# An expert layer computed on every token, changed to one computed on the chosen experts' rows, in a whole decoder layer

## The chip, the core and the metric

The kernel runs on one core of a Trainium2 chip, in one launch. The metric is device time in microseconds (us) of one execution. The core's engines run at the same time and meet at semaphores: TensorE (PE in the profile; PEld is its loading of weights), VectorE (DVE), ScalarE (ACT), GpSimd (POOL) and SyncE (SP), which here only issues transfers (DMAs).

## The reference

The input is 32 sequences of 256 tokens of width 256. Each goes through three residual layers: self attention with rotary embedding (16 heads of 64), cross attention to a context of 256 tokens (16 heads of 64, with a mask on the query rows), and a mixture of 8 experts:

```python
x = x + attention(layernorm(x))
x = x + cross_attention(layernorm(x), ctx, mask)
h = layernorm(x)
probs = softmax(h @ Wg)                       # 8 experts
top_vals, top_idx = top_k(probs, 2)
gates = top_vals / sum(top_vals)
expert_out = einsum('th,ehd->etd', h, We) + be
x = x + sum over the two chosen experts of gate * expert_out
```

All is fp32. The kernel splits each operand of a projection into a high and a low part (`fp32r`) and sums three products of them (`pieces`).

## The kernel before

One sequence is one batch, `b`. The program is a software pipeline: `body(b)` goes through 36 slots, and each engine has its own list of what it does in a slot, in an order that is written out by hand. An engine executes its list strictly in that order. A head takes one slot: self heads 0 to 15 in slots 0 to 15, cross heads 16 to 31 in slots 20 to 35. In slots 16 to 19 no head begins (`DRAIN`); there the self attention's output is projected, added, normalised and turned.

What a head does: `scores` (PE, two heads in every even slot, into two PSUM banks), `row_maximum` (DVE), `exponentials` (ACT), `reciprocal` (DVE), the multiplication by it (POOL, L1150, one slot later), `turn_probs` (PE, L648, two slots later), `pT_out` (ACT) and `values` (PE, L665). `scores` of the next two heads waits until the exponentials of the last one are done (in cross attention until DVE has copied the scores). Every fourth head, `oT_out`, `oT_low` and `project` (PE, L690) follow.

Everything else is a unit in the table `UNITS`: slot, kind, index, the batch it works for (0, the next or the one before) and whether ACT and DVE treat it in that slot or the next (`NOW`, `LATE`). Kinds Q, K and V are projections; the Q and K of self attention also take three operations of POOL each (L1158, L1162, L1139), in slots 30 to 9. L1, L2 and L3 are the turns after the three normalisations, LG the gate logits, GT and BI the expert biases.

EX is the expert layer of the batch before, as eight units in slots 8 to 19: each multiplies 128 tokens by the matrices of two experts (`tile_product`, L546, six matmuls of 512 columns), and DVE adds both halves, weighted by `gates`, to `x1` (L1021). All 8 experts are computed on all 256 tokens, and `gates` is zero for the six that were not chosen. BI adds the biases, and SP stores `x1` to the output. The matrices of all experts lie in SBUF from batch 0 on.

SP's list in a batch is short: the context in slot 9, the mask, two small loads, the output in slot 20 and the next input in slot 22. After batch 31 comes `body(32)`, with no heads: only the expert layer of batch 31.

## Time and profile before

| | |
|---|---|
| median of 3 runs | 3581.41 us (3578.99 to 3582.03) |
| span of the profiled execution, first to last instruction | 3581.8 us |
| that execution's own time | not given apart from the span; the page has only the span |
| PE busy | 3501.3 us, 98% |
| DVE, ACT, POOL busy | 66%, 62%, 59% |
| one steady batch | 109.3 us: the same operation (`rstd` of slot 24) begins at 1000.02 and at 1109.33 us |

A steady batch in the trace: slot 24 begins at about 1000 us, slot 0 at about 1036, slot 8 at about 1057, slot 12 at about 1069, slot 16 at about 1078 and slot 20 at about 1097. In a row of the page, `xN` is a count, the two numbers behind the first bar are the busy time in us and the mean duration in ns, and behind the second bar stands the idle time of the engine before them and who ended it. In a timeline row come the start and the duration in us (of all, where it has a count), the engine, the line and the operation, and in brackets the engine's idle time before it and who ended it. A windows row has the length of the stretch, then the busy time of PE, PEld, DVE, ACT and POOL, the granted clock as a share of 2.4 GHz, the DMA share and GB/s.

### The profile page before, as it was taken

How to read it: one execution, taken by the hardware profiler on the slowest of the kernel's cores; microseconds unless marked ns; L12 is line 12 of the kernel's file. 1: busy time of each engine (PE TensorE's matmuls, PEld its weight loads, DVE VectorE, ACT ScalarE, POOL GpSimd, SP SyncE). 2: the span in 40 equal slices, each digit the busy share in tenths (PEclk: the TensorE clock that was granted, in tenths of full speed). 3: DMA queues.
4: the chain of work that ended last, by engine and by line, in shares of the span. 5: the costliest groups of instructions: out<-in, count | busy, mean ns of one | idle time of the engine just before them, and what ended most of it. 6: DMA issues, size and time to landing. Idle time of an engine off the chain costs nothing.

```text
span 3581.8 us, 80997 instructions
## 1 busy us (share of the span) xinstructions
PE 3501.3 (98%) x28992; PEld 2949.8 (82%) x28992; DVE 2358.7 (66%) x7401; ACT 2220.8 (62%) x6442; POOL 2121.2 (59%) x1928
## 2 busy tenths in 40 slices
PE   6899999999999999999999999999999999999998
PEld 5788888888888888888888888888888888888886
DVE  6666667666666666676666666666766667666665
ACT  5666666666666666666666666666666666666663
POOL 5555676555665556765556755566655567555662
PEclk8999999999999999999999999999999999999999
DMA  3100000000000000000000000000000000000000
GB/s 98 37 10 13 10 10 10 10 13 12 7 10 12 9 12 10 9 10 10 12 12 7 10 12 10 12 10 9 10 10 12 12 7 12 11 10 12 13 6 8
DMA packets 46796, 47.44 MB, mean 13 GB/s; under 512 B 8256, under 2 KB 43328, under 8 KB 46400
## 3 DMA queue, kind: packets, MB, share of 16 engines
q1 hardware_dynamic: 45696, 41.99, 4.0%
q8 instruction: 236, 3.87, 0.4%
q14 instruction: 160, 1.31, 0.1%
q10 hardware_dynamic: 704, 0.27, 0.0%
HBM read 33.86 MB, written 8.39 MB: 12 GB/s over the span
## 4 chain that ended last, share of the span: by engine, by line
PE 89%; DVE 5%; ACT 2%; issue 2%; POOL 2%; DMA 0%; ACTq 0%; POOLq 0%; DVEq 0%
PE unit_ps L536 19%; PE pT_ps L648 14%; PE oT_ps L665 14%; PE score_ps L632 11%; PE unit_ps L524 10%; PE wo_ps L690 10%; PE unit_ps L546 8%; DVE x L1021 1%; ACT probs L798 1%; POOL probs L1150 1%; DVE probs L936 1%; PE unit_ps L555 1%; DVE bn L863 1%; DVE x_in L1029 1%; ACT v_sb L744 1%
## 5 line engine op out<-in xcount | busy, mean ns | idle before, releaser
L1150 POOL TENSOR_TENSOR probs<-probs,inv_sum 128x512 f32<-128x512 f32 x1024 | 1062.1, 1041 | 956.4 <-DVE inv_sum L919 956.3
L787 ACT ACTIVATE pT<-pT_ps 128x512 f32<-128x512 f32 x1024 | 606.2, 594 | 136.1 <-PE pT_ps L648 135.5
L798 ACT ACTIVATE probs<-probs,neg_max 128x256 f32<-128x256 f32 x1024 | 508.9, 500 | 276.4 <-DVE probs L936 276.4
L648 PE MATMUL pT_ps<-ident,probs 128*128 128x128 f32 x4096 | 634.0, 279 | 13.2 <-POOL probs L1150 12.5
L648 PEld LDWEIGHTS pT_ps<-ident,probs 128*128 128x128 f32 x4096 | 451.8, 141 | 221.8 <-issue 204.0
L798 ACT ACTIVATE probs<-score_ps,neg_max 128x256 f32<-128x256 f32 x1024 | 476.6, 476 | 179.1 <-DVE neg_max L925 179.1
L665 PE MATMUL oT_ps<-pT,v_sb 128*64 128x256 f32 x4096 | 556.0, 392 | 4.4 <-ACT pT L787 4.0
L936 DVE TENSOR_SCALAR_CACHE_REDUCE probs<-score_ps,mask_add 128x256 f32<-128x256 f32 x1024 | 433.4, 480 | 104.8 <-PE score_ps L632 101.9
L536 PE MATMUL unit_ps<-xs_hi,w_lo 128*128 128x256 f32 x1536 | 460.1, 300 | 9.3 <-DVE swap L972 7.8
L536 PE MATMUL unit_ps<-xs_hi,w_hi 128*128 128x256 f32 x1536 | 436.6, 284 | 0.0
L536 PE MATMUL unit_ps<-xs_lo,w_hi 128*128 128x256 f32 x1536 | 436.1, 284 | 0.0
L632 PE MATMUL score_ps<-k_hi,q_both 64*128 64x256 f32 x4096 | 387.1, 278 | 0.0
L925 DVE TENSOR_REDUCE neg_max<-score_ps 128x2 f32<-128x512 f32 x512 | 328.2, 682 | 88.7 <-PE score_ps L632 84.4
L665 PEld LDWEIGHTS oT_ps<-pT,v_sb 128*64 128x64 f32 x4096 | 248.8, 136 | 148.1 <-ACT pT L787 5.2
L632 PE MATMUL score_ps<-k_lo,q_both 64*128 64x256 f32 x2048 | 343.0, 331 | 15.6 <-ACT probs L798 8.7
L1162 POOL TENSOR_TENSOR rope<-rope,swap 128x512 f32<-128x512 f32 x256 | 331.4, 1295 | 20.1
L1158 POOL TENSOR_TENSOR swap<-swap,sin_sb 128x512 f32<-128x512 f32 x256 | 332.3, 1298 | 13.3 <-DVE swap L972 13.3
L1021 DVE SCALAR_TENSOR_TENSOR x<-unit_ps,gates,x 128x256 f32<-128x256 f32 x512 | 247.3, 483 | 109.3 <-PE unit_ps L546 98.8
L632 PEld LDWEIGHTS score_ps<-k_hi,q_both 64*128 64x128 f32 x4096 | 316.9, 186 | 0.0
L807 ACT ACTIVATE oT_hi<-oT_ps 128x512 fp32r<-128x512 f32 x256 | 153.1, 598 | 264.1 <-PE oT_ps L665 264.1
L744 ACT ACTIVATE v_sb<-unit_ps 128x512 f32<-128x512 f32 x256 | 152.4, 595 | 262.5 <-PE unit_ps L524 261.3
L536 PEld LDWEIGHTS unit_ps<-xs_hi,w_lo 128*128 128x128 f32 x1536 | 296.0, 193 | 20.9 <-issue 12.2
(121 smaller groups left out, 8573.0 us busy)
## 6 DMA issues: line engine op xcount, KB each, us to landing
x_in<-dram_x SPq DMA_DIRECT2D x32, 256.0 KB, 2.7
xn<-dram_ctx SPq DMA_DIRECT2D x32, 256.0 KB, 2.7
layer_out<-x SPq DMA_DIRECT2D x32, 256.0 KB, 2.2
swap<-dram_bout SPq DMA_DIRECT2D x32, 128.0 KB, 3.1
rope<-dram_be SPq DMA_DIRECT2D x32, 64.0 KB, 2.9
rope<-dram_we SPq DMA_DIRECT2D x5, 256.0 KB, 2.8
probs<-dram_sk SPq DMA_DIRECT2D x4, 256.0 KB, 5.1
x<-dram_cq SPq DMA_DIRECT2D x4, 256.0 KB, 3.2
```

The lines of the kernel that those rows point to most:

```text
L524: last = nc.tensor.matmul(ps[:, t * GW:(t + 1) * GW], a[:, c, t * P:(t + 1) * P], w[:, m, cols:cols + GW], start=n == 0, stop=n == 3 * NC - 1)
L536: last = nc.tensor.matmul(ps[:, j * T:(j + 1) * T], w[:, m, cols:cols + P], a[:, c, :], start=n == 0, stop=n == 3 * NC - 1)
L632: last = nc.tensor.matmul(score_ps[(s + i) % 2][:, t * T:(t + 1) * T], q_both[own, g % 2, q, cols], k[own, g % 2, c, :], start=n == 0, sto ...
L648: last = nc.tensor.transpose(pT_ps[s % 2][:, k * T + t * P:k * T + (t + 1) * P], probs[:, hs % P_BUFS, t, k * P:(k + 1) * P], ident[:])
L665: last = nc.tensor.matmul(oT_ps[i * HD:(i + 1) * HD, (hl // 2) * T:(hl // 2 + 1) * T], v_sb[:, g % 2, k, (hl + i) * HD:(hl + i + 1) * HD], ...
L690: last = nc.tensor.matmul(wo_ps[:, t * D:(t + 1) * D], o[:, c, t * P:(t + 1) * P], w[:, m, cols:cols + D], start=gg == 0 and t == 0 and c ...
L787: nc.scalar.activation(flat(pT[:, s % 2, :, :]), pT_ps[s % 2][:], ACT.Copy).then_inc(pT_ready.sem, 1)
L798: last = nc.scalar.activation(dst, src, ACT.Exp, bias=neg_max[:, h % STATS, t:t + 1], scale=1.0 if h < H else -1.0, accum_out=row_sum[:, h ...
L936: last = nc.vector.tensor_scalar(probs[:, s % P_BUFS, t, :], ps[:, t * T:(t + 1) * T], mask_add[:, t:t + 1], None, ALU.subtract, ALU.min, ...
L1150: nc.gpsimd.tensor_tensor(weights, weights, inv.unsqueeze(2).to_broadcast([P, NT, T]), ALU.mult).then_inc(probs_ready.sem, 1)
L1158: nc.gpsimd.tensor_tensor(swap[:], swap[:], sin_sb[:].unsqueeze(1).to_broadcast([P, NC, T]), ALU.mult).then_inc(sin_done.sem, 1)
L1162: nc.gpsimd.tensor_tensor(rope[:, n % 2, :, :], rope[:, n % 2, :, :], swap[:], ALU.add).then_inc(roped.sem, 1)
```

## The change

The expert layer no longer works batch by batch. The sequences fall into five groups (0 to 8, 9 to 17, 18 to 25, 26 to 29, 30 and 31). For each sequence:

- after the gates, DVE makes a one-hot table, PE counts by two small matmuls how many earlier tokens of the group chose each expert (unit RK, slot 11), and DVE makes from it the row of each of a token's two copies in a DRAM table that has a stretch of rows for each expert (`rows`);
- POOL scatters the normalised tokens to these rows, by four indirect DMAs of 128 rows of 1 KB in slot 13 (`scatter`);
- `x1` (with the biases) is stored to a DRAM tensor `x1_all` where it was stored to the output.

When a group is complete, DVE makes a list of its tiles of 128 rows with one expert each (`list_tiles`, slot 14). Two tiles are a pair; the groups have 22, 22, 20, 12 and 8 pairs, 84 in all. SP loads a pair's rows and its two expert matrices (512 KB each) with four DMAs, whose addresses it reads from the list; PE turns the rows (TT), ACT and DVE split them, PE multiplies (TM, twelve matmuls of 256 columns), ACT copies out, and SP stores the result rows with two DMAs. 69 pairs stand in batches 10 to 15, 19 to 24 and 27 to 31 (three, four or five in each), five in `body(32)`, and ten behind it.

For the sums, SP loads `x1` back, POOL gathers for each half of a sequence the 128 rows of either choice (two indirect DMAs), DVE adds both, weighted, to `x1_back`, and SP stores that to the output. `y_rows` and `x1_back` have one buffer each. 22 sequences are summed in batches 16 to 29 and 31, four in `body(32)`, and six behind it. A batch's first sum gathers in slots 0 and 4, its second in 8 and 12, the third in 20 and 24, the fourth in 28 and 32.

In batches 0, 2, 4 and 6, SP clears the four DRAM tables of 19,456 rows of 1 KB, in 36 DMAs each. SBUF no longer holds the expert matrices; they are split and stored to DRAM in batch 0.

```diff
+GROUPS = ((0, 9), (9, 18), (18, 26), (26, 30), (30, 32))
+CAP = max(e - b for b, e in GROUPS) * T
+ROWS = E * (CAP + P)
...
+LIST_AT = 14
+PAIRS_IN = {10: (0, 4), 11: (0, 4), 12: (0, 4), 13: (0, 4), 14: (0, 3), 15: (0, 3),
+            19: (1, 4), 20: (1, 4), 21: (1, 4), 22: (1, 4), 23: (1, 3), 24: (1, 3),
+            27: (2, 5), 28: (2, 5), 29: (2, 5), 30: (2, 5), 31: (3, 5), 32: (3, 5)}
+SUMS_IN = {**{b: 1 for b in range(16, 25)}, 25: 2, 26: 2, 27: 2, 28: 2, 29: 1, 31: 4, 32: 4}
+GATHER_AT = (0, 4, 8, 12, 20, 24, 28, 32)
+
...
-    9: [("EX", 1, -1, LATE)],
+    8: [("V", 2, 0, LATE), ("TT", 0, 0, NOW)],
+    9: [("TM", 0, 0, LATE)],
     10: [("V", 3, 0, NOW)],
-    11: [],
-    13: [],
-    14: [("EX", 3, -1, NOW)],
+    11: [("RK", 0, -1, LATE), ("TT", 1, 0, NOW)],
+    12: [("TM", 1, 0, LATE)],
+    13: [("TT", 2, 0, NOW)],
+    14: [("TM", 2, 0, LATE)],
     15: [],
     16: [],
-    17: [("K", 4, 0, NOW), ("EX", 4, -1, NOW)],
-    18: [("GT", 0, -1, NOW), ("EX", 5, -1, NOW), ("EX", 6, -1, LATE), ("V", 4, 0, NOW), ("L2", 0, 0, LATE)],
-    19: [("K", 5, 0, NOW), ("Q", 4, 0, NOW), ("EX", 7, -1, NOW)],
+    17: [("K", 4, 0, NOW), ("TT", 3, 0, NOW)],
+    18: [("GT", 0, -1, NOW), ("TM", 3, 0, NOW), ("TT", 4, 0, NOW), ("V", 4, 0, NOW), ("L2", 0, 0, LATE)],
+    19: [("K", 5, 0, NOW), ("Q", 4, 0, NOW), ("TM", 4, 0, NOW)],
     20: [("BI", 0, -1, LATE)],
     21: [("Q", 5, 0, LATE)],
...
+            def clear_rows(i, s):
+
+                blocks = range(s * ROWS // P // SLOTS, (s + 1) * ROWS // P // SLOTS)
+                sp.wait_ge(consts, 8)
+                sp.dma_start((x_rows + y_all)[i][blocks[0] * P:(blocks[-1] + 1) * P, :].rearrange("(n p) d -> p n d", p=P),
+                             y_tile[:, 0, :].unsqueeze(1).to_broadcast([P, len(blocks), D])).then_inc(cleared[i], 16)
...
+            def load_pair(n):
+
+                g = group_of_pair(n)
+                sp.wait_ge(list_ready, g + 1)
+                if n >= 2:
+                    sp.wait_ge(tiles_done, n - 1)
+                for i in range(2):
+                    at = tile_of_pair(n) + i
+                    sp.dma_start(x_tile[:, n % 2, i, :],
+                                 x_rows[g % 2][bass.ds(row_at(n, i), P), :]).then_inc(x_tile_in[n % 2], 16)
+                    expert = sp.value_load(tile_list[at:at + 1, g, 1:2], min_val=0, max_val=E - 1)
+                    sp.dma_start(w_tile[:, n % 2, i, :, :, :].rearrange("p h c n -> p (h c n)").bitcast(F32),
+                                 we_all[bass.ds(expert, 1), :, :].rearrange("e p n -> p (e n)")) \
+                        .then_inc(w_tile_in[n % 2], 16)
...
+            def store_pair(n):
+
+                g = group_of_pair(n)
+                if g >= 2:
+                    sp.wait_ge(half_done, NT * GROUPS[g - 2][1])
+                sp.wait_ge(y_ready, n + 1)
+                for i in range(2):
+                    sp.dma_start(y_all[g % 2][bass.ds(row_at(n, i), P), :], y_tile[:, i, :]).then_inc(y_stored[g % 2], 16)
+
+            def load_x1(q):
+
+                sp.wait_ge(stored.sem, stored.at(q, 0, 1))
+                if q:
+                    sp.wait_ge(out_stored, 16 * q)
+                sp.dma_start(x1_back[:], x1_all[q].rearrange("(t p) d -> p t d", p=P)).then_inc(x1_back_in, 16)
+
+            def store_sum(q):
+
+                sp.wait_ge(half_done, NT * (q + 1))
+                sp.dma_start(out_d[q].rearrange("(t p) d -> p t d", p=P), x1_back[:]).then_inc(out_stored, 16)
+
+            sp.dma_start(places[:], places_d).then_inc(small_in, 16)
             sp.dma_start(x_in[:], x_d[0].rearrange("(t p) d -> p t d", p=P)).then_inc(x_loaded.sem, 16)
...
+                        clear_rows(b // 2, s)
+                    for j in range(E // 2):
+                        if (b, s) == (0, LATER[weights_split("e", j) - 1 - WHOLE][0] + 1):
+                            store_experts(j)
+                    for i in range(len(SUMS.get(b, ()))):
+                        if s == GATHER_AT[2 * i]:
+                            load_x1(SUMS[b][i])
+                    for i, n in enumerate(PAIRS.get(b, ())):
+                        if s == AT["tile products"][i] + 1:
+                            store_pair(n)
+                            if n + 2 < pairs_through(group_of_pair(n)):
+                                load_pair(n + 2)
+                    if s == LIST_AT + 2 and b < B:
+                        first_pairs(b)
+                    for i in range(len(SUMS.get(b, ()))):
+                        if s == min(GATHER_AT[2 * i + 1] + 3, SLOTS - 1):
+                            store_sum(SUMS[b][i])
                     if s == AT["context"] - 2 and exists(b, 0):
 
                         sp.wait_ge(xs_turned.sem, xs_turned.at(b, 0, 1))
-                        if exists(b, -1):
...
                             .then_inc(x_loaded.sem, 16)
 
             bodies(sp, body)
-            sp.wait_ge(stored.sem, 16 * B)
+            first_pairs(B)
+            for n in LAST_PAIRS:
+                if n - 2 >= LAST_PAIRS[0]:
+                    store_pair(n - 2)
+                if group_of_pair(n) == len(GROUPS) - 1:
+                    load_pair(n)
+            for n in LAST_PAIRS[-2:]:
+                store_pair(n)
+            for n in LAST_SUMS:
+                load_x1(n)
+                store_sum(n)
+            sp.wait_ge(out_stored, 16 * B)
 
...
+            def pair_turns(ps, n):
+
+                pe.wait_ge(x_tile_in[n % 2], 32 * (n // 2 + 1))
+                turn(ps, x_tile[:, n % 2, :, :]).then_inc(tiles_turned, 1)
+
+            def pair_products(ps, n):
+
+                pe.wait_ge(tile_lo_ready, n + 1)
+                pe.wait_ge(w_tile_in[n % 2], 32 * (n // 2 + 1))
+                for i in range(2):
+                    k = 0
+                    for c in range(NC):
+                        w = w_tile[:, n % 2, i, :, c, :]
+                        for a, half in ((xf_lo, 1), (xf_hi, 0), (xf_hi, 1)):
+                            last = nc.tensor.matmul(ps[:, i * D:(i + 1) * D], a[:, c, i * P:(i + 1) * P],
+                                                    w[:, half, :], start=k == 0, stop=k == 3 * NC - 1)
+                            k += 1
+                last.then_inc(tiles_done, 1)
...
@@ -720,6 +948,14 @@
                     pe.wait_ge(wg_split, 2)
 
             bodies(pe, body)
+            pe.wait_ge(bias_added.sem, bias_added.at(B - 1, 0, 1))
+            pe.wait_ge(rank_read.sem, rank_read.at(B - 1, 0, 1))
+            pe.wait_ge(y_ready, LAST_PAIRS[0])
+            for n in LAST_PAIRS:
+                pe.wait_ge(tile_lo_ready, n)
+                pair_turns(unit_ps[0], n)
+                pe.wait_ge(y_ready, n)
+                pair_products(unit_ps[1], n)
 
 
...
+            def tile_out(ps, n):
+
+                act.wait_ge(tiles_done, n + 1)
+                if n:
+                    act.wait_ge(*pairs_stored(n - 1))
+                else:
+                    for i in range(4):
+                        act.wait_ge(cleared[i], 16 * SLOTS)
+                nc.scalar.activation(flat(y_tile[:]), ps, ACT.Copy).then_inc(y_ready, 1)
...
+            def add_half(q, t):
+
+                dve.wait_ge(x1_back_in, 16 * (q + 1))
+                dve.wait_ge(y_rows_in, 32 * (NT * q + t + 1))
+                x1_t = x1_back[:, t, :]
+                nc.vector.scalar_tensor_tensor(x1_t, y_rows[:, 0, :], share_of[:, q, t, 0:1], x1_t,
+                                               ALU.mult, ALU.add).then_inc(half_step, 1)
+                dve.wait_ge(half_step, NT * q + t + 1)
+                nc.vector.scalar_tensor_tensor(x1_t, y_rows[:, 1, :], share_of[:, q, t, 1:2], x1_t,
+                                               ALU.mult, ALU.add).then_inc(half_done, 1)
...
+            def scatter(q):
+
+                g = group_of(q)
+                if g >= 2:
+                    pool.wait_ge(tiles_turned, pairs_through(g - 2))
+                if g < 2 and q == GROUPS[g][0]:
+                    pool.wait_ge(cleared[g], 16 * SLOTS)
+                pool.wait_ge(rows_ready.sem, rows_ready.at(q, 0, 1))
+                for t in range(NT):
+                    for i in range(2):
+                        nc.gpsimd.indirect_dma_start(
+                            out=x_rows[g % 2], out_offset=bass.IndirectOffsetOnAxis(ap=row_of[:, q, t, i:i + 1], axis=0),
+                            in_=xm[:, t, :], in_offset=None).then_inc(scattered[g % 2], 16)
+
+            def gather(q, t):
+
+                g = group_of(q)
+                pool.wait_ge(*pairs_stored(pairs_through(g) - 1))
+                if NT * q + t:
+                    pool.wait_ge(half_done, NT * q + t)
+                for i in range(2):
+                    nc.gpsimd.indirect_dma_start(
+                        out=y_rows[:, i, :], out_offset=None, in_=y_all[g % 2],
+                        in_offset=bass.IndirectOffsetOnAxis(ap=row_of[:, q, t, i:i + 1], axis=0)).then_inc(y_rows_in, 16)
...
+                    if s == LIST_AT - 1 and exists(b, -1):
+                        scatter(b - 1)
+                    for i in range(2 * len(SUMS.get(b, ()))):
+                        if s == GATHER_AT[i]:
+                            gather(SUMS[b][i // 2], i % 2)
 
             bodies(pool, body)
+            for q in LAST_SUMS:
+                for t in range(NT):
+                    gather(q, t)
 
 
```

How the instructions move. PE in slots 12 to 14 of a batch before (`oT_ps` are the values, `pT_ps` the turned probabilities, `we` the expert unit):

```order
L665 MATMUL oT_ps<-pT,v_sb 64x256 x4
L648 MATMUL pT_ps<-ident,probs 128x128 x4
L546 MATMUL unit_ps<-we_hi,xf_lo 128x512
L546 MATMUL unit_ps<-we_lo,xf_hi 128x512
L546 MATMUL unit_ps<-we_hi,xf_hi 128x512
L546 MATMUL unit_ps<-we_hi,xf_lo 128x512
L546 MATMUL unit_ps<-we_lo,xf_hi 128x512
L546 MATMUL unit_ps<-we_hi,xf_hi 128x512
L648 MATMUL pT_ps<-ident,probs 128x128 x4
```

The same place in a batch without pairs:

```order
L893 MATMUL oT_ps<-pT,v_sb 64x256 x4
L876 MATMUL pT_ps<-ident,probs 128x128 x8
L860 MATMUL score_ps<-k_lo,q_both 128x256 x2
```

The expert unit is gone, the turns of two slots follow one another, and the next scores stand right behind them. In a batch with pairs:

```order
L893 MATMUL oT_ps<-pT,v_sb 64x256 x4
L876 MATMUL pT_ps<-ident,probs 128x128 x4
L765 MATMUL unit_ps<-w_tile,xf_lo 128x256
L765 MATMUL unit_ps<-w_tile,xf_hi 128x256 x2
L765 MATMUL unit_ps<-w_tile,xf_lo 128x256
L765 MATMUL unit_ps<-w_tile,xf_hi 128x256 x2
L765 MATMUL unit_ps<-w_tile,xf_lo 128x256
L765 MATMUL unit_ps<-w_tile,xf_hi 128x256 x2
L765 MATMUL unit_ps<-w_tile,xf_lo 128x256
L765 MATMUL unit_ps<-w_tile,xf_hi 128x256 x2
L876 MATMUL pT_ps<-ident,probs 128x128 x4
L774 MATMUL unit_ps<-ident,x_tile 128x128 x4
```

Here a product of a pair stands where the expert unit was, and a turn of the next pair's rows ahead of the next scores.

POOL in slots 2 to 4 of a batch before (`probs` is the multiplication of a head, `swap`, `rope`, `k_lo` and `q_both` are the rotary embedding, `rstd` the third normalisation):

```order
L1162 TENSOR_TENSOR rope<-rope,swap 128x512
L1150 TENSOR_TENSOR probs<-probs,inv_sum 128x512
L1139 TENSOR_TENSOR q_both<-rope,q_both 128x512
L1150 TENSOR_TENSOR probs<-probs,inv_sum 128x512
L1158 TENSOR_TENSOR swap<-swap,sin_sb 128x512
L1162 TENSOR_TENSOR rope<-rope,swap 128x512
L1126 TENSOR_TENSOR rstd<-var_eps,neg_half 128x2
L1150 TENSOR_TENSOR probs<-probs,inv_sum 128x512
```

The same place in a batch with a sum:

```order
L1512 TENSOR_TENSOR q_both<-rope,q_both 128x512
L1523 TENSOR_TENSOR probs<-probs,inv_sum 128x512
L1531 TENSOR_TENSOR swap<-swap,sin_sb 128x512
L1535 TENSOR_TENSOR rope<-rope,swap 128x512
L1499 TENSOR_TENSOR rstd<-var_eps,neg_half 128x2
L1492 DMA y_rows<-y_all0,row_of 128x256 x2
L1523 TENSOR_TENSOR probs<-probs,inv_sum 128x512
L1512 TENSOR_TENSOR k_lo<-rope,k_hi 128x512
```

Two indirect gathers stand between `rstd` and the next head. POOL in slots 10 to 18 (`ct_lo` is the low part of the context), before and now:

```order
L1150 TENSOR_TENSOR probs<-probs,inv_sum 128x512 x2
L1169 TENSOR_TENSOR ct_lo<-xn,ct_hi 128x512
L1150 TENSOR_TENSOR probs<-probs,inv_sum 128x512 x5
L1126 TENSOR_TENSOR rstd<-var_eps,neg_half 128x2
```

```order
L1523 TENSOR_TENSOR probs<-probs,inv_sum 128x512 x2
L1542 TENSOR_TENSOR ct_lo<-xn,ct_hi 128x512
L1523 TENSOR_TENSOR probs<-probs,inv_sum 128x512 x2
L1481 DMA x_rows1<-xm,row_of 19456x256 x4
L1523 TENSOR_TENSOR probs<-probs,inv_sum 128x512 x3
L1499 TENSOR_TENSOR rstd<-var_eps,neg_half 128x2
```

Four indirect scatters stand between the multiplications of heads 12 and 13. What SP does for one pair of another (store two tiles, of which the second is shown, and load two, of which the first is shown; TENSOR_LOAD reads an address from the list):

```order
L599 TENSOR_LOAD tile_list
L599 ISA x2
L633 ISA
L633 DMA y_all0<-y_tile 128x256
L599 TENSOR_LOAD tile_list
L599 ISA x2
L609 ISA
L609 DMA x_tile<-x_rows0 128x256
L611 TENSOR_LOAD tile_list
L611 ISA x2
L612 ISA
L612 DMA w_tile<-we_all 128x1024
```

Before, SP had seven such rows in a whole batch; now each pair is six reads of the list and six DMAs.

## Rows read from the trace of the kernel before

**Rows 1.** The page, parts 1 and 2: busy time; granted clock.
```profile
PE 3501.3 (98%) x28992; PEld 2949.8 (82%) x28992; DVE 2358.7 (66%) x7401; ACT 2220.8 (62%) x6442; POOL 2121.2 (59%) x1928
...
PEclk8999999999999999999999999999999999999999
```

**Rows 2.** Windows: slots 0 to 7, slots 8 to 15, the end.
```profile
1036.00:1057.20 21.20, 21.20 (x196) 18.71 (x196) 16.42 (x45) 14.90 (x44) 20.66 (x20) 1.00 0.05 14
1057.20:1078.40 21.20, 21.18 (x168) 16.94 (x163) 14.83 (x45) 14.91 (x47) 12.06 (x11) 1.00 0.04 10
3542.00:3581.80 39.80, 25.14 (x106) 18.32 (x104) 15.71 (x50) 3.51 (x10) 1.59 (x2) 0.83 0.02 7
```

**Rows 3.** Chain of waits, slots 8 to 11: start, us, what.
```profile
1059.89 1.40 PE unit_ps L546 x6
...
1061.29 0.44 PE pT_ps L648 x4
...
1067.49 1.43 PE wo_ps L690 x12
```

**Rows 4.** Timeline, slots 9 and 10: last exponential, next scores.
```profile
1060.87 0.47 ACT L798 ACTIVATE probs<-score_ps,neg_max 128x256 f32<-128x256 f32 x1
...
1063.04 0.39 PE L632 MATMUL score_ps<-k_lo,q_both 64*128 64x256 f32 x2
```

**Rows 5.** Timeline, slots 12 and 13: one turn of the head loop.
```profile
1068.86 0.39 PE L632 MATMUL score_ps<-k_lo,q_both 64*128 64x256 f32 x2
...
1069.87 1.29 DVE L925 TENSOR_REDUCE neg_max<-score_ps 128x2 f32<-128x512 f32 x2 [1.06 <-PE score_ps L632]
...
1072.85 0.22 ACT L798 ACTIVATION_READ_ACCUMULATOR probs<-score_ps,neg_max 128x1 f32 x1
...
1073.19 0.38 PE L632 MATMUL score_ps<-k_lo,q_both 64*128 64x256 f32 x2
```

**Rows 6.** Timeline, slots 18 to 20: second normalisation to first cross scores.
```profile
1088.98 0.70 POOL L1126 TENSOR_TENSOR rstd<-var_eps,neg_half 128x2 f32<-128x2 f32 x1 [8.54 <-DVE var_eps L871]
...
1091.53 0.66 PE L555 MATMUL unit_ps<-ident,xn 128*128 128x128 f32 x4
...
1096.06 0.69 DVE L948 SCALAR_TENSOR_TENSOR q_both<-unit_ps,q_both 128x512 fp32r<-128x512 f32 x1 [0.74 <-ACT q_both L767]
...
1096.95 0.39 PE L632 MATMUL score_ps<-k_lo,q_both 64*128 64x256 f32 x2
```

**Rows 7.** POOL timeline: one operation of slot 2, then slots 12 to 16.
```profile
1043.06 1.29 POOL L1139 TENSOR_TENSOR q_both<-rope,q_both 128x512 fp32r<-128x512 f32 x1
...
1074.02 2.04 POOL L1150 TENSOR_TENSOR probs<-probs,inv_sum 128x512 f32<-128x512 f32 x2 [2.06 <-DVE inv_sum L919]
...
1078.41 2.04 POOL L1150 TENSOR_TENSOR probs<-probs,inv_sum 128x512 f32<-128x512 f32 x2 [2.35 <-DVE inv_sum L919]
```

**Rows 8.** Waits of PE over the span.
```profile
PE pT_ps L648 <- POOL probs L1150: 12.5, 37, 1.9
```

**Rows 9.** The page, part 6 (us to landing), and SP timeline (issue).
```profile
x_in<-dram_x SPq DMA_DIRECT2D x32, 256.0 KB, 2.7
...
layer_out<-x SPq DMA_DIRECT2D x32, 256.0 KB, 2.2
...
1100.88 0.40 SPq L494 DMA_DIRECT2D layer_out<-x  x1
```

**Rows 10.** The page, part 5: the adds of the experts.
```profile
L1021 DVE SCALAR_TENSOR_TENSOR x<-unit_ps,gates,x 128x256 f32<-128x256 f32 x512 | 247.3, 483 | 109.3 <-PE unit_ps L546 98.8
```

**Rows 11.** SP timeline: the last store.
```profile
3579.25 0.38 SPq L494 DMA_DIRECT2D layer_out<-x  x1
```

**Rows 12.** DVE rows by line: min/median/max ns.
```profile
L878 DVE TENSOR_SCALAR xn<-x_in,mean_var,rstd x128: 400/409/699, 9.7 to 3495.5; 128x256 f32<-128x256 f32 x128
...
L878 DVE TENSOR_SCALAR xn<-x,mean_var,rstd x64: 406/1053/1361, 173.9 to 3554.2; 128x256 f32<-128x256 f32 x64
...
L887 DVE TENSOR_TENSOR g_prob<-g_exp,g_inv x32: 175/1106/1123, 183.6 to 3560.8; 128x16 f32<-128x16 f32 x32
```

335 lines of the change are left out of this document (259 added, 76 removed).

## The prediction

> **What bounds the kernel now.** I read the busy times first: PE 98%, every other engine at 66% or less, the granted clock at full from the second slice on [rows 1]. That says "PE-bound", and if it were the whole story, every matmul removed would be time saved. So I asked by stretches, and then by the chain, what stands behind PE. In slots 0 to 7 of a steady batch POOL is busy 20.66 of 21.20 us [rows 2]: it paces these slots together with PE, and PE already waits for its multiplied heads at moments [rows 8]. In slots 8 to 15 POOL has room (12.06 us), and expert units fill PE [rows 2, 3]. The chain of waits gives those units their length, but it names whatever was last, and PE is nearly always last by a hair. Two places show what comes next without them:
>
> The head loop. Scores of slot 12 begin at 1068.86, DVE's two maxima end at 1071.16, ACT's last exponential at 1073.07, scores of slot 14 begin at 1073.19 [rows 5]. One turn is 4.33 us, and the next scores start 0.12 us after what they wait for. The expert unit in it (1.40 us) hides in a wait.
>
> The drain, slots 16 to 19: `rstd` 1088.98, turn of the normalised rows 1091.53, low part of Q ends 1096.75, first cross scores 1096.95 [rows 6]. This too is a chain of single operations, with PE filling.
>
> **What the change removes.** Eight units of 1.40 us a batch [rows 3], 11.2 us, in 31 batches: 347 us of PE. Those in slots 12 and 14 and four in the drain cover waits. In the drain only the turn can come earlier: the norm ends at about 1090.6 and the turn stands behind other products until 1091.53, so 0.9 us. In slots 8 and 9, 2.8 us of units stand between the turns; the last exponential ends at 1061.34 and the scores begin at 1063.04 [rows 4], so 1.6 us at most by ACT, and DVE spends slot 8 in the gate table, which gets longer. Bounds 0.4 and 2.8; I take 1.1, near ACT's. Together 2.0 us in each of the 14 batches without pairs: **-28 us**. In the 17 batches with pairs, a pair costs PE 1.43 + 0.44 = 1.87 us [rows 3], and ACT 1.2 us in the very loop above: I count these batches at no gain, and the term's bounds are the rival with PE (-218) and 0.
>
> **What it adds on POOL.** No indirect DMA is in the trace, so its time on POOL, c, is the unknown on which most hangs. Below lies SP's issue of a transfer, 0.40 us [rows 9]; above, I double POOL's longest ordinary operation of 1.29 us [rows 7], 2.6. I take that operation itself, c = 1.3, since both are one software loop over 128 partitions' worth of work (that is a guess).
>
> Scatter, slot 13, 31 times. Heads 12 and 13 are multiplied from 1074.02, heads 14 and 15 until 1080.45 [rows 7]. Without the expert add, head 12's reciprocal is there at about 1072.3, its multiplication ends at 1073.4; then four scatters and three multiplications of 1.04 end at 1076.5 + 4c. Late by 4c - 3.9, which is 1.3 us, and the values of heads 14 and 15, which start the drain's chain, wait for it: 31 x 1.3 = **+40 us** (0 at c = 0.4, +202 at 2.6).
>
> Gathers. A batch's first sum puts two gathers behind slot 0 and two behind slot 4, where POOL has nothing free: 4c. Behind the waiting POOL stand the rotary operations and the next heads, and PE waits for both. 15 batches have one. Five have a second sum in slots 8 and 12, of which I let about 2.2 us hide in POOL's room; batch 31 has two more in slots 20 to 32, at 4c each. In all 15 x 4c + 5 x (4c - 2.2) + 8c = 88c - 11: **+103 us** at 1.3 (27 at 0.4, where the second sums are free, and 218 at 2.6). DVE's adds (0.48 us each, four a sum [rows 10]) replace sixteen a batch. They stand three slots behind their gathers, so a landing of 2 to 3 us is over when DVE comes to them; were it not, the next maxima and with them ACT would stand behind the wait. I count them at nothing.
>
> The Trainium skill, "SBUF — State Buffer", section on who shares the engine ports, says that POOL and a DVE operation with two SBUF inputs or in a two-port mode take a shared port pair by turns, whole instructions at a time, and that descriptors of a DMA from POOL wait as well. Rows show the first half: the same normalisation takes 409 ns away from POOL and 1053 beside it, a 128x16 product 175 or 1106 [rows 12]. By the rule each add of a sum would take up to 0.6 us more, the difference of those rows, 22 x 4 x 0.6 = 53 us over my sum, which the range below holds. No row shows the half about descriptors. The Trainium skill, "DMA: Bandwidth & Descriptors", gives about 1 us to the first byte for a DMA issued on GpSimd; were c that 1.0, the sum would be 3813, an estimate from its figure.
>
> **What it adds on SP.** x1 is stored in slot 20 at 1100.88 [rows 9], and DVE's next use of it in slot 22 waits. With five pairs (batches 27 to 31) a pair's store and load, twelve instructions, stand ahead of it: I count 3 us in each. Clearing in four batches moves 0.55 MB a slot through the same queue, ahead of inputs: 1 to 2 us a batch and again at the start. Together **+20 us** (0 to 60).
>
> **What it adds behind the last batch.** Here nothing covers anything, and buffers are single; already before, the clock granted in the last 40 us is 0.83 on the mean, with POOL busy 1.59 us and ACT 3.51 [rows 2]: a chain of single operations. A half sum is two gathers (2c), landing 2.2 us [rows 9], two dependent adds 1.05 [rows 10]: 2c + 3.25 = 5.85 us; the next gather waits for it. Before, the last store is issued at 3579.25 [rows 11]. In `body(32)`, five pairs, each waiting for the store of the one before, and then three half sums end some 30 us later than that. Ten pairs follow, eight of them with loads of 1.25 MB: six address reads and six DMAs of SP at 0.4 us or more each, and 2.7 us landing [rows 9], against which two buffers are held: 7 us a pair, 8 x 7 + 6 = 62 us. Twelve half sums, 12 x 5.85 = 70, a load and a store at the ends, 6. Sum **+168 us** (141 at c = 0.4, 207 at 2.6; pairs at 12 us instead of 7 would add 50).
>
> Sum: 3581.8 - 28 + 40 + 103 + 168 + 20 = 3885. The span of the profiled execution is within 0.4 us of the median, 3581.4, so nothing is scaled.
>
> **Rivals.**
> 1. The issue is cheap, c = 0.4. For: SP's is. Against: SP has a queue of its own kind, POOL computes addresses. 3582 - 28 + 0 + 27 + 141 + 20 = 3742.
> 2. The issue is dear, c = 2.6. For: 256 rows' addresses instead of a plain pattern. 3582 - 28 + 202 + 218 + 207 + 20 = 4201.
> 3. The end is dear, c as taken: address reads on SP of 2 us, pairs at 15 us and sums at 10 us. Then behind the last batch 40 + 126 + 126 = 292 in place of 168, and 40 more in slot 20 and slot 13: 4050.
> 4. Faster: PE is the bound after all. If scores of slots 10 to 14 followed PE, 14 batches would save 11.2 us and 17 save 3.6, 218 us in all. For: 98%. Against: 0.12 us between exponential and scores [rows 5]. With the cheap issue: 3582 - 218 + 0 + 27 + 141 + 20 = 3552. It decides from a saving of 6 us a batch, with c under 0.5.
>
> **How the numbers follow.** My forecast 0.52, rival 1 0.18, rival 2 0.12, rival 3 0.12, rival 4 0.06. Faster by more than 0.2% (about what a measurement tells from no change) only in rival 4: 0.06. The same needs a mean of them: 0.01. Slower 0.93. The forecast's own range is 3790 to 3990 (c from 1.0 to 1.8, pairs from 5 to 10 us); reaching to rival 1's 3742 and rival 3's 4050, 3735 to 4080 leaves rival 2 and rival 4 outside.
>
> **What would show it.** Right: batches without pairs or sums run within 3 us of 109.3; a batch with a sum is about 5 us longer than one without; PE's largest wait is for POOL's multiplied heads in slots 0 to 8; after the last `x1` store over 130 us pass with PE mostly idle and its granted clock at the lower level, 1.2 GHz. The interval between two gathers of one half is c. Wrong: batches of 100 us or less in 1 to 9 (rival 4), no growth of batches 16 to 24 over 10 to 15 (rival 1), POOL busy or issuing 8 us or more in slot 13 (rival 2), SP late for the `x1` store by over 5 us (rival 3).

## The result, and the profile after

The changed kernel takes 4061.95 us in the median (4055.91 to 4072.65), the kernel before 3581.59 us beside it; the ratio is 1.1346, 95% interval 1.1329 to 1.1363. It is slower by 480 us, where 303 were forecast: 4062 lies inside the range, but above the forecast's own 3790 to 3990. The profiled execution's span is 4062.7 us.

The head of its page, which answers to [rows 1]:

```profile
PE 3427.6 (84%) x28864; PEld 2917.2 (72%) x28864; DVE 2228.5 (55%) x7380; ACT 2316.0 (57%) x6612; POOL 2376.8 (59%) x2189
PEclk8999999999999999999999999999999999999855
```

PE is busy 74 us less in a span that is 481 us longer, so more work on PE is not what makes the kernel slower. To see where the time went I took the start of POOL's root (`rstd`) for slot 24 of each batch as a mark; two of them enclose one period, and period n ends at the mark of batch n. In the kernel before a period is 109.3 us, the first 111.0.

```
periods (mark of slot 24 to mark of slot 24)       mean us  over before   in all
1, 3, 5, 7, 8, 9   no pair, no sum, no clearing      111.6       2.0        12
2, 4, 6            with clearing                     117.3       8.0        24
10 to 15           pairs                             113.8       4.5        27
16 to 18           one sum                           119.4      10.1        30
19 to 24           pairs, one sum                    119.4      10.1        60
25, 26             two sums                          123.2      13.9        28
27 to 30           five pairs, up to two sums        128.8      19.4        78
31                 five pairs, four sums                                    29
from the last mark to the end, 221.8 instead of 28.7                       193
```

The sum is 481 us, the spans' difference. Behind the last batch 193 us stand against 168 forecast; inside the loop 288 against 135, twice as much.

POOL in slot 13 of batch 8 (start, duration, line; in brackets the idle time before), the answer to [rows 7]:

```profile
990.31 1.04 POOL L1523 TENSOR_TENSOR probs<-probs,inv_sum 128x512 f32<-128x512 f32 x1
992.01 1.04 POOL L1523 TENSOR_TENSOR probs<-probs,inv_sum 128x512 f32<-128x512 f32 x1 [0.66 <-DVE inv_sum L1264]
993.22 1.06 POOL L1481 DMA_INDIRECT x_rows<-xm,row_of  x1 [0.17 <-issue]
994.59 0.96 POOL L1481 DMA_INDIRECT x_rows<-xm,row_of  x1 [0.30 <-issue]
995.85 0.96 POOL L1481 DMA_INDIRECT x_rows<-xm,row_of  x1 [0.30 <-issue]
997.12 0.96 POOL L1481 DMA_INDIRECT x_rows<-xm,row_of  x1 [0.31 <-issue]
998.10 3.04 POOL L1523 TENSOR_TENSOR probs<-probs,inv_sum 128x512 f32<-128x512 f32 x3
```

From one indirect DMA to the next pass 1.26 to 1.37 us: c was right. Heads 13, 14 and 15 are multiplied in one go behind them.

PE's waits of the whole span (total, times, longest), the answer to [rows 8]:

```profile
PE pT_ps L876 <- POOL probs L1523: 231.6, 164, 10.2
PE score_ps L860 <- ACT probs L1055: 56.3, 49, 11.2
PE unit_ps L774 <- DVE xn L1141: 56.3, 25, 8.6
```

12.5 us before, 231.6 now: POOL's late heads are what PE waits for. The forecast put these waits in slots 0 to 8; in a batch without a sum they stand behind the scatter, 3.61 us in one piece in batch 7. What comes behind such a wait is in the windows around the second gather of batch 16, in slot 4:

```profile
1880.00:1884.60 4.60, 1.72 (x18) 1.02 (x17) 3.32 (x9) 2.73 (x7) 4.08 (x5) 1.00 0.20 59
1884.60:1888.00 3.40, 3.40 (x19) 3.40 (x18) 0.77 (x2) 2.10 (x6) 3.32 (x4) 0.51 0.00 0
1888.00:1895.00 7.00, 7.00 (x65) 6.32 (x65) 5.14 (x14) 3.30 (x11) 5.52 (x5) 1.00 0.18 55
```

While POOL issues, PE is busy 1.72 of 4.60 us, and for the next 3.4 us it is granted 1.2 instead of 2.4 GHz: 19 products in 3.4 us, against 65 in the 7.0 us after them. Before, the clock was at its upper level from 107 us to 3547 us without a break; now it falls in 26 of the 30 periods.

The queue of SP in slots 19 to 22 of batch 28, and DVE behind it (answers to [rows 9]):

```profile
3395.03 1.47 SPq L633 DMA_DIRECT2D y_all<-y_tile  x2
3397.33 0.36 SPq L609 DMA_DIRECT2D x_tile<-x_rows  x1
3398.46 0.36 SPq L612 DMA_DIRECT2D w_tile<-we_all  x1
3399.59 0.34 SPq L609 DMA_DIRECT2D x_tile<-x_rows  x1
3400.69 0.34 SPq L612 DMA_DIRECT2D w_tile<-we_all  x1
3401.08 0.43 SPq L693 DMA_DIRECT2D x_all<-x  x1
```

```profile
3405.94 0.69 DVE L1430 TENSOR_TENSOR x<-x_in,swap 128x512 f32<-128x512 f32 x1 [5.63 <-DMA x_all<-x]
```

From one DMA at an address read from the list to the next SP takes 1.1 us, so the store of x1 is issued 6 us after the pair's stores, and DVE waits 5.63 us. Of these the last 4.9 us pass between the issue of that store (3401.08) and DVE's start (3405.94).

The end, in three windows: slot 4 of the last batch's experts to the end of `body(32)`, the ten pairs, the twelve half sums (answers to [rows 2]):

```profile
3840.00:3914.00 74.00, 26.48 (x104) 21.53 (x104) 18.31 (x68) 7.84 (x16) 18.01 (x19) 0.53 0.51 164
3914.00:3986.00 72.00, 36.39 (x156) 31.07 (x156) 7.01 (x11) 11.34 (x19) 1.89 (x2) 0.59 0.55 186
3986.00:4062.70 76.70, 0.00 (x0) 0.00 (x0) 11.62 (x24) 0.00 (x0) 20.82 (x22) 0.50 0.26 82
```

Pairs and sums together are 149 us of an otherwise empty chip, where 132 were forecast.

### The profile page after: what moved, and what is told of

It is laid out like the page before. It is cut to its first block, busy times and chain, and to the rows that moved or that the text cites. A ratio compares the mean times of both kernels' runs of the same rounds, so it can differ in the third digit from the quotient of the medians.

```text
span 4062.7 us, 84690 instructions
## 1 busy us (share of the span) xinstructions
PE 3427.6 (84%) x28864; PEld 2917.2 (72%) x28864; DVE 2228.5 (55%) x7380; ACT 2316.0 (57%) x6612; POOL 2376.8 (59%) x2189
## 4 chain that ended last, share of the span: by engine, by line
PE 54%; POOL 20%; issue 8%; DVE 8%; ACT 5%; DMA 3%; SPq 2%; another core or an unknown queue 0%; POOLq 0%; ACTq 0%; DVEq 0%
PE unit_ps L746 14%; PE pT_ps L876 9%; PE oT_ps L893 8%; POOL probs L1523 8%; PE wo_ps L918 7%; PE score_ps L860 7%; PE unit_ps L734 5%; POOL rope L1535 2%; POOL swap L1531 2%; ACT probs L1055 2%; POOL y_rows L1492 2%; POOL x_rows L1481 2%; PE unit_ps L774 2%; POOL k_lo L1512 2%; PE unit_ps L765 2%
## 5 line engine op out<-in xcount | busy, mean ns | idle before, releaser
L876 PE MATMUL pT_ps<-ident,probs 128*128 128x128 f32 x4096 | 648.6, 284 | 233.5 <-POOL probs L1523 231.6
L893 PE MATMUL oT_ps<-pT,v_sb 128*64 128x256 f32 x4096 | 566.0, 398 | 10.2 <-ACT pT L1044 9.8
L746 PE MATMUL unit_ps<-xs_hi,w_lo 128*128 128x256 f32 x1536 | 473.8, 308 | 6.3 <-DVE swap L1317 3.6
L918 PE MATMUL wo_ps<-w_hi,oT_lo 128*128 128x256 f32 x1024 | 314.9, 308 | 24.3 <-DVE oT_lo L1369 24.3
L860 PEld LDWEIGHTS score_ps<-k_lo,q_both 64*128 64x128 f32 x2048 | 194.7, 185 | 174.8 <-ACT probs L1055 73.2
L746 PEld LDWEIGHTS unit_ps<-xs_hi,w_lo 128*128 128x128 f32 x1536 | 304.4, 198 | 21.1 <-issue 12.1
L1499 POOL TENSOR_TENSOR rstd<-var_eps,neg_half 128x2 f32<-128x2 f32 x96 | 67.9, 707 | 427.5 <-DVE var_eps L1134 427.5
```

What stands on the lines that cost most here:

```text
L746: last = nc.tensor.matmul(ps[:, j * T:(j + 1) * T], w[:, m, cols:cols + P], a[:, c, :], start=n == 0, stop=n == 3 * NC - 1)
L860: last = nc.tensor.matmul(score_ps[(s + i) % 2][:, t * T:(t + 1) * T], q_both[own, g % 2, q, cols], k[own, g % 2, c, :], start=n == 0, sto ...
L876: last = nc.tensor.transpose(pT_ps[s % 2][:, k * T + t * P:k * T + (t + 1) * P], probs[:, hs % P_BUFS, t, k * P:(k + 1) * P], ident[:])
L893: last = nc.tensor.matmul(oT_ps[i * HD:(i + 1) * HD, (hl // 2) * T:(hl // 2 + 1) * T], v_sb[:, g % 2, k, (hl + i) * HD:(hl + i + 1) * HD], ...
L918: last = nc.tensor.matmul(wo_ps[:, t * D:(t + 1) * D], o[:, c, t * P:(t + 1) * P], w[:, m, cols:cols + D], start=gg == 0 and t == 0 and c ...
```

## The experiments

I took the change apart and added the parts again one at a time. Kernel names are those of the runs. The kernel before, timed again beside each group of runs, took 3580.4 us.

**r1_removal**: nothing of the experts but the ranks.

```
-  if s == LIST_AT - 1 and exists(b, -1): scatter(b - 1)
-  PAIRS = {...}; SUMS = {...}; clear_rows(b // 2, s)
+  PAIRS = {};  SUMS = {};  x1 stored to layer_out
```

(Here and in some of the code below lines are shortened; `...` stands for what is left out.)

> The changed kernel with only its removal: no expert products at all (no clearing, scatter, pairs, gathers or sums; x1 with its bias part is stored as the output), the ranks and row numbers still made. By the prediction's first step 2.0 us a batch go: 3582 - 31 x 2 = 3520, with the new rank operations on DVE perhaps 3530. Rival (PE is the bound): 11.2 us a batch go, 3582 - 347 = 3235. Rival (granted clock): PE, left without work in slots 12 to 19, falls to 1.2 GHz there in most batches, and the drain gives the gain back: 3560 to 3600, with spells at the lower clock in over half of the batches, and none in slots 24 to 4.

Measured 3531.45 us, ratio 0.9862 (0.9846 to 0.9878). 49 us are gone: the step was right in kind and size, and PE is not the bound. Slots 4 to 18 take 39.8 instead of 41.1 us and slots 18 to 24 take 19.3 instead of 20.3. 25 spells at the lower clock stand in 19 of the 30 periods, all behind the root of slot 18; a batch with one spell takes 108.1 us, one without 106.85. So the lower clock takes back 1.2 us of the 2.5 gained where it falls, and about 30 us in all.

```profile
1069.80:1073.00 3.20, 0.79 (x6) 0.62 (x5) 1.69 (x8) 0.60 (x1) 0.70 (x1) 0.95 0.00 0
1073.00:1076.90 3.90, 3.90 (x23) 3.90 (x22) 0.69 (x1) 1.20 (x2) 0.00 (x0) 0.60 0.00 0
```

These windows are at the norm of slot 18: PE is busy 0.79 of 3.20 us, then its granted clock is 0.60 on the mean, that is mostly 1.2 GHz.

**r2_removal_fill**: the same, with unread products in the eight old places.

```
+  for i in range(2):
+      for k in range(6):
+          nc.tensor.matmul(unit_ps[at % 2][:, i * D:(i + 1) * D], w_hi[:, 1, k * P:(k + 1) * P],
+                           w_hi[:, 0, 0:D], start=k == 0, stop=k == 5)
```

> As the removal alone, but with twelve matrix products of 256 columns, whose result nobody reads, in each of the eight places where an expert unit stood, in batches 1 to 31. If PE's work there was spare (the prediction), and the clock plays no part, this stands where the removal alone stands, within 15 us, or up to 60 us above it if the 2 us a batch were really PE's. If the granted clock matters, it is faster than the removal alone by 20 us or more, though it does more, and has hardly a spell at the lower clock. If PE is the bound, 3582.

Measured 3564.99, ratio 0.9958 (0.9941 to 0.9975). The clock never falls in the loop, and still each period is 109.0 us, 34 us in all above the removal alone. So the expert units did cost time themselves (2.2 us a batch where the clock holds), keeping the clock up with idle work doesn't pay, and the DVE additions that went with the units were worth little (109.0 against 109.3).

**r3_scatter13** and **r4_scatter16**: the removal plus the scatter, in slot 13 as in the change, and in slot 16.

```
-  if s == LIST_AT - 1 and exists(b, -1):
+  if s == 16 and exists(b, -1):
       scatter(b - 1)
```

> The removal alone plus the 128 indirect DMAs of the scatter in slot 13 (no clearing, pairs, gathers or sums). Each takes POOL 1.27 us. By the prediction's step 4 x 1.27 - 3.9 = 1.2 us a batch more than the removal alone: +37 us, without more time at the lower clock. Rival: PE's wait for the late heads brings the lower clock, which costs 1 to 2 us more a batch: +60 to +100 us, and the spells at 1.2 GHz stand right behind slot 13 and at its drain.

> The same scatter in slot 16, behind the last head's multiplication, where POOL otherwise stands idle for 11.4 us before it takes the norm's root (no clearing, pairs, gathers or sums). Both theories: within 10 us of the removal alone. If instead the descriptors or the writes themselves cost (DVE's port, the DMA queues), it stands as far above as with the scatter in slot 13.

Measured 3661.31 (1.0235, 1.0215 to 1.0254) and 3530.01 (0.9858, 0.9842 to 0.9875). The same 128 DMAs cost 130 us in one place and nothing three slots later. POOL from the multiplication of head 13 to the root of slot 18, without the scatter, with it in slot 13, and with it in slot 16:

```profile
948.11 1.04 POOL L1510 TENSOR_TENSOR probs<-probs,inv_sum 128x512 f32<-128x512 f32 x1 [0.28 <-DVE inv_sum L1253]
951.71 1.04 POOL L1510 TENSOR_TENSOR probs<-probs,inv_sum 128x512 f32<-128x512 f32 x1 [2.56 <-DVE inv_sum L1253]
953.11 1.04 POOL L1510 TENSOR_TENSOR probs<-probs,inv_sum 128x512 f32<-128x512 f32 x1 [0.36 <-DVE inv_sum L1253]
963.09 0.70 POOL L1486 TENSOR_TENSOR rstd<-var_eps,neg_half 128x2 f32<-128x2 f32 x1 [8.94 <-DVE var_eps L1123]
```

```profile
984.83 1.07 POOL L1468 DMA_INDIRECT x_rows<-xm,row_of  x1 [0.17 <-issue]
...
988.74 0.96 POOL L1468 DMA_INDIRECT x_rows<-xm,row_of  x1 [0.30 <-issue]
989.72 3.03 POOL L1510 TENSOR_TENSOR probs<-probs,inv_sum 128x512 f32<-128x512 f32 x3
1002.59 0.72 POOL L1486 TENSOR_TENSOR rstd<-var_eps,neg_half 128x2 f32<-128x2 f32 x1 [9.84 <-DVE var_eps L1123]
```

```profile
955.35 1.04 POOL L1510 TENSOR_TENSOR probs<-probs,inv_sum 128x512 f32<-128x512 f32 x1 [0.36 <-DVE inv_sum L1253]
956.56 1.07 POOL L1468 DMA_INDIRECT x_rows<-xm,row_of  x1 [0.17 <-issue]
...
960.46 0.96 POOL L1468 DMA_INDIRECT x_rows<-xm,row_of  x1 [0.30 <-issue]
965.35 0.72 POOL L1486 TENSOR_TENSOR rstd<-var_eps,neg_half 128x2 f32<-128x2 f32 x1 [3.92 <-DVE var_eps L1123]
```

Counted from the mark of slot 4 (923.30, 960.14 and 925.54 us), head 13 is multiplied at 24.8 us without the scatter and at 29.6 with it in slot 13, 4.8 us late; the last head ends 1.8 us late, about what I reckoned (4c - 3.9 = 1.2); and the root comes at 42.5 instead of 39.8, 2.7 us late even in this batch, where the clock holds. I had priced the last head only, but head 13's turn, its values and its projection wait as well, and PE can't do them all at once afterwards. In 24 of the 30 periods a spell at the lower clock follows PE's wait (36 spells in the loop), and these periods are mostly 5.4 to 6.2 us over 106.85 instead of 2.7. In slot 16 POOL would idle 8.94 us, and the 5.1 us of the scatter fit in.

**r5_full_sc16**: the complete changed kernel with that one move (the edit of r4, and SP's wait for a group's last scatter in slot 17 instead of 16).

> The changed kernel, complete, with its scatter in slot 16 instead of slot 13 (and SP's wait for it at a group's end in slot 17 instead of 16). If the late heads of slot 13, and the lower clock that follows them, cost every batch what they cost in the kernel that has only the scatter (4.2 us), 31 x 4.2 = 130 us go: 3930. Rival: in the 17 batches with pairs the pair products fill PE's wait for the late heads, so that only the 14 others gain: 14 x 4.2 = 59 us, 4000. If the scatter were no matter in company, 4062.

Measured 4034.18 (1.1271, 1.1252 to 1.1290): only 28 us less, below both expectations. Periods 1 to 8, without pairs or sums, fall to 106.8 to 109.9 us, nearly as in r4. The gain is lost in three places. In periods 10 to 15, with pairs, slots 4 to 18 keep 43.9 to 47.3 us (44.9 to 47.9 in the changed kernel). Periods 19 to 24, with pairs and a sum, even get longer, 122.2 us on the mean instead of 119.4, 17 us in all; why isn't settled. And in periods 9, 18 and 26, where a group ends, slots 18 to 24 take 26 to 29 us instead of 19 to 21, 24 us in all: my own edit made SP wait in slot 17 and issue the first two pairs' loads ahead of what the drain needs (see r11). Period 30, where the fourth group ends, takes 30 to 31 us there in both kernels. Without my edit's 24 us the time would be about 4010 (an estimate from these periods), near the rival's 4000: the batches with pairs gain next to nothing.

**r6_full_sc16_sp**: x1's store ahead of the pair in slot 20.

```
   if kind == "BI" and exists(b, -1): ... sp.dma_start(x1_all[b - 1] ..., x1[:])
+  for i, n in enumerate(PAIRS.get(b, ())):
+      if s == AT["tile products"][i] + 1:
+          store_pair(n); load_pair(n + 2)
```

> As the last one, and SP issues the store of x1 in slot 20 before the pair's store and loads of that slot instead of behind them. That concerns only the six batches with five pairs. DVE waits 5.6 us for that store in the changed kernel: 4 to 5 us a batch in batches 27 to 32, 20 to 30 us less than the scatter's move alone. If the store's DMA itself is slow beside 1.25 MB of loads, and not its place in the queue, under 8 us.

Measured 4023.92 (1.1242, 1.1223 to 1.1261): 10 us less, half of what I expected. Slots 18 to 24 of batches 27 to 29 stay at 24.6 to 25.9 us (25.1, 24.8, 25.6 without the edit); the gain is in batch 31 and what follows. The trace shows where the wait went (batch 28, SP and DVE):

```profile
3371.76 0.43 SPq L700 DMA_DIRECT2D x_in<-dram_x  x1
```

```profile
3376.46 0.75 DVE L1126 BATCH_NORM_STATS2 bn<-x_in 128x6 f32<-128x256 f32 x2 [4.75 <-DMA x_in<-dram_x]
```

Now SP issues the load of the next input right behind the pair's six transfers, and DVE waits 4.75 us for it, nearly all of it after the issue. Without the edit (r5) SP issued that load at 3378.42, 5.7 us after the store of x1, and DVE used it 2.7 us later. So the wait passed from the store to the load that comes next, and with it most of the gain.

**r7_full_sc16_sums**: gathers where POOL idles.

```
 GATHER_AT = (0, 4, 8, 12, 20, 24, 28, 32)
+def gather_at(b):
+    n = len(SUMS.get(b, ()))
+    return {1: (17, 19), 2: (8, 12, 17, 19)}.get(n, GATHER_AT)
```

> As the last one, and the sum of a batch with one sum gathers in slots 17 and 19 (added in 18 and 22) instead of slots 0 and 4, and of a batch with two sums in 8, 12, 17, 19 instead of 0, 4, 8, 12. By the prediction's step a sum in slots 0 and 4 costs 4c = 5.1 us where POOL has nothing free, and in slots 17 and 19, where it has, nothing: 15 x 5.1 = 76 us less; by the periods of the changed kernel's trace (8.1 us a sum) up to 120. Rival: the adds (1.0 us each) stand in the drain's chain on DVE and cost there what they cost on POOL before: 30 us less or nothing.

Measured 3956.39 (1.1058, 1.1039 to 1.1076): 68 us less. Periods 16 and 17 (one sum, no pair) are 109.1 and 109.9 instead of 116.3 and 115.2 us, and slots 24 to 4 of periods 16 to 26 are back at 47.1 to 47.8 from 50.6 to 52.4. The sum is free beside idle slots; beside pairs it keeps part of its cost (periods 19 to 24: 117.6 on the mean, 113.1 in r8 without sums).

**r8_pairs16**: clearing, scatter in slot 16 and pairs, no sums.

> Clearing, scatter in slot 16 and all pairs, but no gathers and no sums (x1 with its bias part is stored as the output). Above the scatter alone in slot 16 (3530) it shows what the pairs and clearing cost. By the prediction's steps: pairs nothing in the loop but what the removal gave (17 x 2.4 = 41), clearing and SP 20, pairs behind the last batch 62 to 75: 3660. Rival, from the periods of batches 10 to 15 of the changed kernel: a batch with pairs costs 3 us more than that, 50 us: 3710.

Measured 3795.15 (1.0594, 1.0576 to 1.0612): 265 us above r4. My move of SP's wait is in it, about 24 us by r5, so about 241 are left for pairs and clearing, above both expectations. The sums, with their transfers, are all that r5 has beyond it, and add 239. The head loop shows why pairs cost so much. Scores of slots 12 and 14 in r4 (batch 13):

```profile
1486.23 0.38 PE L853 MATMUL score_ps<-k_lo,q_both 64*128 64x256 f32 x2
...
1490.49 0.38 PE L853 MATMUL score_ps<-k_lo,q_both 64*128 64x256 f32 x2 [0.98 <-ACT probs L1044]
```

and in r8, same batch:

```profile
1529.54 0.61 ACT L1007 ACTIVATE xf_hi<-unit_ps 128x512 fp32r<-128x512 f32 x1
1529.92 0.39 PE L860 MATMUL score_ps<-k_lo,q_both 64*128 64x256 f32 x2
1530.18 0.69 DVE L1287 TENSOR_TENSOR xf_lo<-unit_ps,xf_hi 128x512 fp32r<-128x512 f32 x1 [3.52 <-ACT xf_hi L1007]
...
1533.94 0.60 PE L876 MATMUL pT_ps<-ident,probs 128*128 128x128 f32 x4
1534.13 0.60 ACT L1017 ACTIVATE y_tile<-unit_ps 128x512 f32<-128x512 f32 x1 [0.91 <-PE unit_ps L765]
1534.63 0.47 ACT L1055 ACTIVATE probs<-score_ps,neg_max 128x256 f32<-128x256 f32 x1
...
1535.70 0.38 PE L860 MATMUL score_ps<-k_lo,q_both 64*128 64x256 f32 x2 [0.72 <-ACT probs L1055]
1536.00 0.61 ACT L1007 ACTIVATE xf_hi<-unit_ps 128x512 fp32r<-128x512 f32 x1
1536.65 0.69 DVE L1287 TENSOR_TENSOR xf_lo<-unit_ps,xf_hi 128x512 fp32r<-128x512 f32 x1 [3.63 <-ACT xf_hi L1007]
```

A turn takes 5.78 us instead of 4.26. ACT waits 0.91 us for the pair's products (PE runs them ahead of the next head's turn, `pT_ps`), copies them for 0.60, and only then comes to the second head's exponentials. In the next turn DVE's low part ends at 1537.34, and the maxima start behind it, at 1537.40.

**r9_pairs_small** and **r10_pairs_few**: which of the two, the copies or the products?

```
-  nc.scalar.activation(flat(y_tile[:]), ps, ACT.Copy)
+  nc.scalar.activation(flat(y_tile[:])[:, 0:16], ps[:, 0:16], ACT.Copy)
-  for a, half in ((xf_lo, 1), (xf_hi, 0), (xf_hi, 1)):
+  for a, half in ((xf_lo, 1), (xf_hi, 0), (xf_hi, 1))[0:2 if c == 0 else 0]:
```

The first edit (and the same for the pair's high and low part) is r9, the second r10, which keeps four of a pair's twelve products.

> The kernel with clearing, scatter in slot 16 and pairs but no sums (3795), its three copies of a pair (ACT's high part and output, DVE's low part) cut from 512 columns to 16; the pair's results are wrong by that, PE's work is as before. Theory: these copies (0.61 + 0.60 on ACT, 0.69 on DVE) stand in the head loop's chain, ahead of exponentials and maxima, and make a turn of it 5.8 us instead of 4.3. Then slots 4 to 18 of a batch with pairs fall from 43.9 and 47.3 to 41 or less, and the whole by 60 to 100 us: 3700 to 3735. Rival (PE's products delay the next scores): under 20 us less.

> The same kernel with full copies, but four of a pair's twelve products of 512 columns' worth (1.2 us less of PE in each pair; its results are wrong by that). If the copies set the loop's turn, under 20 us less than 3795. If PE does, 4 pairs x 1.2 us in 17 batches and behind the last: 60 to 100 us less.

Measured 3752.96 (1.0482, 1.0465 to 1.0500) and 3756.18 (1.0490, 1.0472 to 1.0507): 42 and 39 us less, of which 9 and 12 stand behind the last mark. Neither theory alone holds. In period 13, where the clock holds in slots 4 to 18, these slots take 43.9 us in r8, 42.3 with small copies, 42.9 with few products, and 39.8 without pairs: copies and products share the chain, as the rows show. Added up (1.6 and 1.0 us) they leave 1.5 of the 4.1 us open: both runs keep part of what they reduce, and none drops the turns of the rows. In r8 the batches from 10 to 15 take 46.8 to 47.4 and 43.9 to 44.7 us there by turns, the longer ones with a spell at the lower clock near their end; why by turns isn't settled.

**r11_full_best**: r7, with SP's wait for a group's last scatter and the group's first loads behind x's load.

```
-  if s == 17 and b < B: first_pairs(b)
+  if s == 23 and b < B: first_pairs(b)
```

> The complete kernel with the scatter in slot 16, x1 stored ahead of the pair, sums in 17 and 19 (3956), and SP's wait for the last scatter and its first two pairs of a group in slot 23, behind x1's store and x's load, instead of slot 17. In batches 9, 18 and 26 slots 18 to 24 took 27 to 28 us instead of 20: 3 x 8 us and one or two more at the next group's end, so 3925 to 3932. If the pairs' loads themselves are what costs, no change.

Measured 3916.72 (1.0941, 1.0923 to 1.0960): 40 us less than r7. Slots 18 to 24 of periods 9, 18 and 26 go from 28.5, 28.1 and 26.8 to 20.5, 20.9 and 20.9, and of period 30 from 32.1 to 19.6. These 12.5 us of period 30 don't come from my edit, because the changed kernel takes 30.1 us there too.

**r12_full_tail**: two buffers for gathered rows and for x1 behind the last batch.

```
+  def gathered(q, t): return x_in if q in LAST_SUMS and t else y_rows
+  def sum_of(q): return xn if q in LAST_SUMS and (q - LAST_SUMS[0]) % 2 else x1_back
```

> As the last one, and behind the last batch the sums have two buffers for the gathered rows and two for x1, so a gather doesn't wait for the addition of the half before it. A half sum takes 6.2 us with one buffer (2 x 1.25 issue, 2.8 landing, 1.0 added, 0.7 to the next issue), and with two POOL's two issues and its wait, 3.3: 12 x 2.9 = 35 us less. If the transfers bound it, under 10 us.

Measured 3887.51 (1.0851, 1.0833 to 1.0869): 29 us less; the stretch behind the last mark goes from 220.9 to 188.0 us. The best complete version found is 174 us under the change and 307 over the kernel before.

## Why the forecast was right in sign and short in size

The runs give each part its measured price. Forecast and measurement are set side by side in the same parts; the forecast's 2.0 us for each of 31 batches stand under removal, and what it did not credit to the 17 batches with pairs (34) under pairs. That term holds pairs, clearing and SP (34 + 20), ten pairs behind the last batch (62), and the rest of `body(32)` and of the ends (18); the sums' term holds 103, 70 and three half sums (18).

```
                              forecast   measured   from
removal                          -62       -49      r1
scatter in slot 13               +40       +52      r5 to after 28, plus 24 of my edit in r5
pairs, clearing, SP             +134      +241      r4 to r8 265, less the same 24
sums                            +191      +239      r8 to r5
together                        +303      +483
```

Alone, the scatter in slot 13 costs 130 us (r3 less r4); in the complete kernel it is worth some 52.

The steps, in the prediction's order:

**The bound.** Right: removing every expert unit gives 1.4%, not 9.7%. Rival 4 is out by r1. A place where an engine starts 0.1 us after another is worth more than a share of 98%.

**c.** Right: 1.26 us against 1.3; rivals 1 and 2 are out. But the value was a guess, and no run tests the reason given for it (one software loop), so that it came out so near is partly luck.

**Scatter.** Right in place, and near in size (52 against 40) for a reason that was incomplete: only the last head was priced, while the first head behind the insertion is late by 4.8 us. Alone the scatter costs 2.7 us a batch where the clock holds and 4.2 on the mean with the spells at the lower clock, 130 us; the total stays near 40 because the batches with pairs lose next to nothing by it (r5), which I hadn't foreseen.

**Sums.** Sized at 4c = 5.1 us each in slots 0 and 4; periods 16 to 18 show 8.1 over those without (period 1 left out), where the sign named was 5 us. POOL's own 5.1 us are in the trace; that the spells behind PE's waits are the rest is argued and not shown by a run.

**Pairs in the loop.** This is the step that failed: "I count these batches at no gain", with 0 as the term's upper bound. The pair's 1.87 us on PE and 1.2 us on ACT were named, and the loop's slack of 0.12 us too, but I set the pairs against the removed units instead of adding them to the chain. A unit put 1.4 us on PE and nothing on ACT. Periods 10 to 15 are 4.5 us over before in the changed kernel and as much in r8, and in r8, without scatter in slot 13 and sums, periods 10 to 15, 19 to 24 and 27 to 31 come to 104 us in place of 0. About 10 of them are SP's first loads of the last group, in period 30. Work in an engine whose next operation is in the chain can only lengthen it or hide; the bound had to lie above 0.

**SP.** Short: 3 us were counted for each batch with five pairs, and slots 18 to 24 of periods 27 to 29 take 24.7 to 26.4 us in r8, against 19.3 to 21.5 in periods 10 to 15. A transfer behind the pair's loads waits for SP's issue and also lands later: 4.7 us from issue to use in r6, 2.7 in r5.

**The end.** Right within 25 us. The stores of the ten pairs follow each other in 6.8 to 8.4 us, 7.4 on the mean (7 forecast), twelve half sums take 76 us, 6.3 each (5.85 forecast). What sets the pairs' pace is mostly SP's issue:

```profile
3963.77 1.47 SPq L633 DMA_DIRECT2D y_all<-y_tile  x2
3966.37 0.36 SPq L609 DMA_DIRECT2D x_tile<-x_rows  x1
3967.51 0.35 SPq L612 DMA_DIRECT2D w_tile<-we_all  x1
3968.63 0.34 SPq L609 DMA_DIRECT2D x_tile<-x_rows  x1
3969.74 0.34 SPq L612 DMA_DIRECT2D w_tile<-we_all  x1
3971.37 0.35 SPq L633 DMA_DIRECT2D y_all<-y_tile  x1
```

One pair's store to the next is 7.60 us here, six transfers at about 1.1 us and a wait. Rival 3 gave 4050, near the measured time, for the wrong reason: its 15 us a pair and 10 us a sum did not happen. Its sign, SP late for the x1 store by over 5 us, did. That the stated range holds 4062 is luck: its upper end was put there for rival 3, and what fills the gap is mostly pairs and sums inside the loop.

**The signs.** Of the nine periods without pairs or sums only 3, 7 and 8 lie within 3 us of 109.3; the scatter and its spells lengthen the others, and clearing three of them.

**DVE's adds at nothing.** Nearly: 22 of the 128 adds took over 0.6 us, all beside a computing operation of POOL (last section).

**What isn't settled:** how the scatter's 52 us divide between late heads and clock (the 24 us of my edit are read from periods and not from a run, so the sum of parts is good to some 10 us); clearing alone, which has no run of its own (periods 2, 4 and 6 are 6.9, 2.7 and 1.1 us longer than in r3, which has the scatter and no clearing); why periods 19 to 24 grow when the scatter moves; and the alternation in batches with pairs. Filling PE in the changed kernel, and pairs in other slots, weren't tried.

## What to carry to other kernels

Before an operation goes into an in-order engine, write down each instruction that stands behind it, and price the lateness of the first, not only of the last. A free place is one where that engine's idle time ahead of its next work is longer than the insertion: the same scatter, alone, cost 130 us in slot 13 and nothing in slot 16. What a part costs alone is not its price in the whole: in the complete kernel that scatter was worth some 52 us. And work that replaces other work must be compared engine by engine: a unit that needs only PE and a pair that needs PE, ACT and DVE are not alike in a loop whose chain runs through all three.

## What the runs showed of the hardware

**In these traces the clock fell behind stretches in which PE had little to do, and not behind each of them.** In the windows shown, PE is busy 1.72 of 4.60 us and 0.79 of 3.20 us, and 3.4 us or so at 1.2 GHz follow. The removal alone, which is faster than before, has 25 such spells, the kernel with the scatter in slot 13 36, the filled one none. In periods 11 and 12 of r1 PE waits 2.4 us at the same place, for the normalised rows behind the root of slot 18; a spell follows in the first and none in the second.

**An addition on DVE waits for whole instructions of POOL.** The first addition of a half sum takes 0.48 us with POOL idle, up to 1.34 beside one of its computing operations, and this, beside two multiplications in a row (POOL, then DVE, of the changed kernel):

```profile
2976.57 2.03 POOL L1523 TENSOR_TENSOR probs<-probs,inv_sum 128x512 f32<-128x512 f32 x2
```

```profile
2976.53 2.36 DVE L1256 SCALAR_TENSOR_TENSOR x_back<-y_rows,share_of,x_back 128x256 f32<-128x256 f32 x1
```

The Trainium skill, "SBUF — State Buffer", section "Who interferes with whom", describes a lock: of an operation of POOL that reads SBUF and one of DVE with two SBUF inputs the first holds the shared ports for its whole length. The trace agrees, and shows more: the add begins 0.1 us before a third operation of POOL ends (at 2976.62), doesn't get in between that and the next, and ends 0.3 us behind both multiplications. So its price is up to 1.9 us and not the 0.6 that I took from one operation. Ten adds that overlap only an indirect DMA of POOL take 0.48 us as with POOL idle. What the section says of descriptors concerns DVE's two-port mode, so these adds don't test it, and no run here was made to.

**An indirect DMA of 128 rows holds POOL for 0.96 us, 1.26 with the gap to the next**, whether it scatters or gathers. From one DMA of SP at an address read from a table in SBUF to the next pass 1.1 us, and 0.5 us from one at a fixed address to the next (3406.66 and 3407.15 us in the changed kernel).
